# P*V with the query tiles split over the array's column halves, and the output projection in row tiles of 64

## What is computed

```python
h = _layernorm(x, ln1_g, ln1_b)
q = (xq @ wq).reshape(B, S, N_HEADS, D_HEAD)
k = (xkv @ wk).reshape(B, T, N_HEADS, D_HEAD)
v = (xkv @ wv).reshape(B, T, N_HEADS, D_HEAD)
attn = jnp.einsum("bihd,bjhd->bhij", q, k) * scale
attn = jax.nn.softmax(attn, axis=-1)
out = jnp.einsum("bhij,bjhd->bihd", attn, v).reshape(B, S, D_ATTN)
x = out @ wo + bo + x
```

## Time and profile before

| | us |
|---|---|
| three timed runs | 1082.41, 1084.62, 1083.84 |
| their median | 1083.84 |
| the profiled execution | 1080.77 |
| its span, first to last instruction | 1079.0 |
| TensorE, matmuls (weight loads) | 1032.9 (837.2) |
| VectorE | 832.9 |
| ScalarE | 623.0 |
| GpSimd | 307.8 |

### The profile page before, as it was taken

The page is one execution under the profiler, slowest core; times in us unless marked ns, Lnnn a source line. Parts: engine busy times, 40 slices in busy tenths (PEclk is TensorE's granted clock), DMA queues, the critical chain, the costliest instruction groups (busy, mean ns, idle before and its releaser), DMA issues.

```text
span 1079.0 us, 28600 instructions
## 1 busy us (share of the span) xinstructions
PE 1032.9 (96%) x12270; PEld 837.2 (78%) x12270; DVE 832.9 (77%) x977; ACT 623.0 (58%) x1120; POOL 307.8 (29%) x280
## 2 busy tenths in 40 slices
PE   6899999999998999999999999998999998999998
PEld 5677777777776777777777777776688888888887
DVE  3598888789989877878888889999868897655433
ACT  2566666566676655666666566676655643443322
POOL 2302332222332223423223222322313357701000
PEclk9999999999999999999999999999999999999999
DMA  7798677556755956665875666598210001100001
GB/s 155 189 219 169 155 151 172 124 114 134 162 114 113 204 114 147 131 133 124 162 159 121 145 122 147 116 218 174 46 60 20 1 20 41 39 1 20 21 1 40
DMA packets 178367, 121.39 MB, mean 113 GB/s; under 512 B 142656, under 2 KB 158528, under 8 KB 173760
## 3 DMA queue, kind: packets, MB, share of 16 engines
q1 hardware_dynamic: 177280, 116.40, 49.4%
q0 software_dynamic: 960, 3.15, 1.0%
HBM read 56.60 MB, written 12.58 MB: 64 GB/s over the span
## 4 chain that ended last, share of the span: by engine, by line
PE 80%; DVE 6%; ACT 5%; issue 4%; POOL 2%; SPq 1%; DMA 1%; DVEq 0%; ACTq 0%; POOLq 0%
PE W L628 21%; PE SC L603 18%; PE W L640 9%; PE SC L692 8%; PE W L578 8%; PE W L702 4%; PE W L588 4%; PE W L868 3%; ACT OTF L954 2%; PE SC L680 2%; DVE PR L1179 2%; DVE nmax L1174 2%; ACT PR L946 1%; PE W L855 1%; POOL PR L515 1%
## 5 line engine op out<-in xcount | busy, mean ns | idle before, releaser
L946 ACT ACTIVATE PR<-SC,nmax 128x1024 f32<-128x1024 f32 x256 | 285.9, 1117 | 225.0 <-DVE nmax L1174 224.5
L1174 DVE TENSOR_REDUCE nmax<-SC 128x1 f32<-128x1024 f32 x256 | 308.0, 1203 | 98.6 <-PE SC L603 97.9
L1179 DVE STREAM_TRANSPOSE PR<-PR 128x1024 f32<-128x1024 f32 x256 | 315.1, 1231 | 0.3 <-ACT PR L946 0.2
L603 PE MATMUL SC<-QKS 128*128 128x512 f32 x1024 | 297.4, 417 | 11.5 <-ACT PR L946 8.0
L464 POOL TENSOR_TENSOR X<-f_raw,X 128x512 f32<-128x512 f32 x128 | 164.8, 1289 | 496.0 <-ACT f_raw L965 495.9
L628 PE MATMUL W<-PR,V 32*64 32x256 f32 x8192 | 240.9, 379 | 1.9 <-issue 1.9
L603 PEld LDWEIGHTS SC<-QKS 128*128 128x128 f32 x1024 | 184.3, 188 | 72.2 <-issue 25.7
L628 PEld LDWEIGHTS W<-PR,V 32*64 32x64 f32 x8192 | 185.8, 132 | 50.8 <-issue 23.9
L640 PE MATMUL W<-wo,OTF 128*128 128x256 f32 x512 | 134.4, 385 | 7.3 <-ACT OTF L954 6.4
L640 PEld LDWEIGHTS W<-wo,OTF 128*128 128x128 f32 x512 | 93.9, 189 | 36.5 <-ACT OTF L954 20.3
L965 ACT ACTIVATE f_raw<-W,rden 128x256 f32<-128x256 f32 x256 | 106.8, 474 | 0.1
(11 more groups left out here) (127 smaller groups left out, 1416.9 us busy)
## 6 DMA issues: line engine op xcount, KB each, us to landing
QKS<-QKT SPq DMA_DIRECT2D x64, 512.0 KB, 6.3
V<-scratch_v SPq DMA_DIRECT2D x128, 256.0 KB, 5.0
QKS<-QKT SPq DMA_DIRECT2D x128, 128.0 KB, 4.9
scratch_v<-VST SPq DMA_DIRECT2D x32, 256.0 KB, 4.7
wo<-in_L_xattn_sa_wo_dram SPq DMA_DIRECT2D x64, 64.0 KB, 3.0
f_raw<-in_L_xattn_ff_w_dram POOLq DMA_DIRECT2D x12, 256.0 KB, 3.4
X<-in_x_dram SPq DMA_DIRECT2D x4, 512.0 KB, 5.0
w_raw<-in_L_xattn_sa_wk_dram SPq DMA_DIRECT2D x16, 128.0 KB, 3.5
```

Of the source, the lines that this page charges most:

```text
L603: last = mm(SC[t % 2][:, cols], QKS[:, 3 * s, t * P:(t + 1) * P], QKS[:, 3 * s + 1 + l, cols], start=(l == 0), stop=(l == 1))
L946: nc.scalar.activation(PR[:, NT * s + t, :], SC[t % 2][:, :], ACT.Exp, bias=nmax[:, t % 4:t % 4 + 1], accum_out=den[:, s, t:t + 1]).then_i ...
L1174: V.tensor_reduce(nmax[:, t % 4:t % 4 + 1], SC[t % 2][:, :], AX, ALU.max, negate=True).then_inc(d_max, 1)
L1179: V.transpose(tile, tile).then_inc(d_tr, 1)
```

## The change

P*V: each key block makes its products twice, once for each column half c of the array, and half c handles the query tiles 4c to 4c+3, 128 columns. All key blocks add up in both halves, so there are no even and odd sums any more: partitions 0 to 63 hold tiles 0 to 3 and partitions 64 to 127 tiles 4 to 7. `OTF` shrinks to 128x512. The projection then takes 64 rows of `OTF` and of `wo2` for each query tile, from partitions 0 to 63 for tiles 0 to 3 and 64 to 127 for tiles 4 to 7. Each of its two steps has four products, tiles t and t+4 in turn, which write two banks. Step 0 stands behind score tile 5, step 1 behind tile 7 and the projections there. ScalarE scales both results of step 0 ahead of the exponentials of tile 6. The pair of tiles that result k holds is now `OUT_TILE[k]`, and behind the last head the banks and waits of `make_vw` follow the new order of the scalings.

```diff
-        OTF = sb("OTF", [P, S])
+        OTF = sb("OTF", [P, BANK])
...
-        MB = [MISC, PV, TP[0], TP[1]]
+        MB = [PV, TP[1], TP[0], MISC]
...
-        STEPS = {5: 0, 6: 1, 7: 2}
-        OUT_BANK = (2, 1, 0, 1)
+        STEPS = {5: 0, 7: 1}
+        OUT_TILE = (0, 4, 2, 6)
+
+        def out_bank(h, n):
+            return (2, 1, 0, 3 if h == HS - 1 else 1)[n]
...
                 for blk in range(*blocks):
-                    cols = slice(DH * (blk % 2), DH * (blk % 2) + DH)
-                    for a in range(4):
-                        rows = slice(Q * a, Q * a + Q)
-                        last = mm(W[cols, a, 0:2 * P], V4[s][rows, blk, :],
-                                  PR[rows, NT * s:NT * s + NT, Q * blk:Q * blk + Q],
-                                  start=(blk < 2), stop=(blk >= NB - 2), tile_position=(Q * a, DH * (blk % 2)))
...
+                    for c in range(2):
+                        cols = slice(DH * c, DH * c + DH)
+                        tiles = slice(NT * s + 4 * c, NT * s + 4 * c + 4)
+                        for a in range(4):
+                            rows = slice(Q * a, Q * a + Q)
+                            last = mm(W[cols, a, 0:P], V4[s][rows, blk, :], PR[rows, tiles, Q * blk:Q * blk + Q],
+                                      start=(blk == 0), stop=(blk == NB - 1), tile_position=(Q * a, DH * c))
...
-            def project_out(h, k):
-                if k == 0:
+            def project_out(h, step):
...
                 for i in range(2):
-                    t = 2 * k + i
-                    last = mm(W[:, OUT_BANK[k], D * i:D * i + D], OTF[:, t * P:(t + 1) * P], wo2[h % 2][:, :],
-                              start=True, stop=True)
-                last.then_inc(s_op, 1)
+                    t = 2 * step + i
+                    for c in range(2):
+                        rows = slice(DH * c, DH * c + DH)
+                        last = mm(W[:, out_bank(h, 2 * step + c), D * i:D * i + D], OTF[rows, t * P:(t + 1) * P],
+                                  wo2[h % 2][rows, :], start=True, stop=True)
+                        if i == 1:
+                            last.then_inc(s_op, 1)
...
-                    if t == 0 and h > 1:
-                        pe.wait_ge(a_op, 4 * (h - 2) + 2)
-                        project_out(h - 2, 3)
...
+                    if h > 0 and t == 7:
+                        pe.wait_ge(a_op, 4 * (h - 1) + 2)
+                        project_out(h - 1, STEPS[t])
...
-                if j > 0:
-                    pe.wait_ge(a_op, 4 * (HS - 1) + (0, 1, 3, 4)[j])
+                pe.wait_ge(a_op, 4 * (HS - 1) + j + 1)
                 make_vw(0, j, MB[j])
...
-                               W[:, :, 0:2 * P].rearrange("p a (t i) -> p a t i", i=Q)).then_inc(a_ot, 1)
+                               W[:, :, 0:P].rearrange("p a (t i) -> p a t i", i=Q)).then_inc(a_ot, 1)
...
-                act.wait_ge(s_op, n + 1)
+                act.wait_ge(s_op, 4 * h + 2 * (k // 2) + 2)
...
-                    if t in (6, 7) and h > 0:
-                        scale_out(h - 1, t - 6)
+                    if t == 6 and h > 0:
+                        scale_out(h - 1, 0)
+                        scale_out(h - 1, 1)
                     if t in (0, 1) and h > 1:
                         scale_out(h - 2, 2 + t)
```

More of the change, by code:

```diff
@@ L462, in add_out @@
                         pool.wait_ge(p_xb, 2 * (h // NH) + 2)
-                    xs = X[:, h // NH, 2 * k:2 * k + 2, :].rearrange("p t d -> p (t d)")
+                    xs = X[:, h // NH, OUT_TILE[k]:OUT_TILE[k] + 2, :].rearrange("p t d -> p (t d)")
                     nc.gpsimd.tensor_tensor(xs, f_raw[:, k % 2, :], xs, ALU.add).then_inc(p_x, 1)
@@ L624, in attend @@
                 for blk in range(*blocks):
-                    cols = slice(DH * (blk % 2), DH * (blk % 2) + DH)
-                    for a in range(4):
-                        rows = slice(Q * a, Q * a + Q)
-                        last = mm(W[cols, a, 0:2 * P], V4[s][rows, blk, :],
-                                  PR[rows, NT * s:NT * s + NT, Q * blk:Q * blk + Q],
-                                  start=(blk < 2), stop=(blk >= NB - 2), tile_position=(Q * a, DH * (blk % 2)))
-                        if blk >= NB - 2:
-                            last.then_inc(s_pv, 1)
-            def project_out(h, k):
-                if k == 0:
+                    for c in range(2):
[5 more added lines that the diff above has]
+                                      start=(blk == 0), stop=(blk == NB - 1), tile_position=(Q * a, DH * c))
+                            if blk == NB - 1:
+                                last.then_inc(s_pv, 1)
+            def project_out(h, step):
+                if step == 0:
                     pe.wait_ge(a_ot, h + 1)
@@ L735, in _ @@
                         attend(h - 1, BURSTS[t])
-                    if h > 0 and t in STEPS:
+                    if h > 0 and t == 5:
                         project_out(h - 1, STEPS[t])
@@ L781, in _ @@
                         turn_wq(i, bank)
-                    if t == 0 and h > 1:
-                        pe.wait_ge(a_op, 4 * (h - 2) + 2)
-                        project_out(h - 2, 3)
-            pe.wait_ge(a_op, 4 * (HS - 2) + 2)
-            project_out(HS - 2, 3)
+                    if h > 0 and t == 7:
+                        pe.wait_ge(a_op, 4 * (h - 1) + 2)
+                        project_out(h - 1, STEPS[t])
             pe.wait_ge(m_kb[0], 16)
@@ L799, in _ @@
             ca_scores(1)
[L800 to L803, removed]
+            for step in range(2):
+                project_out(HS - 1, step)
             pe.wait_ge(m_vb[0], 16)
@@ L965, in scale_out @@
                     done = nc.scalar.mul(f_raw[:, k % 2, D * i:D * i + D],
-                                         W[:, OUT_BANK[k], D * i:D * i + D],
-                                         rden[:, h % 2, 2 * k + i:2 * k + i + 1])
+                                         W[:, out_bank(h, k), D * i:D * i + D],
+                                         rden[:, h % 2, OUT_TILE[k] + i:OUT_TILE[k] + i + 1])
                 done.then_inc(a_op, 1)
```

## The result

The changed kernel takes 1257.3 us, the median of four timed runs, beside 1083.12 for the kernel before on the same chip: a ratio of 1.162 (95% interval 1.158 to 1.167). It is slower by 16%, where the prediction said 2% faster. The profiled execution took 1259.82 us, 1258.0 of them the span.

What follows compares the result with a forecast made beforehand. TensorE was taken to set the pace, with VectorE close behind. From the profiled 1080.8 us, 27 gained in and behind the heads and 7 lost to instruction fetching gave 1060.8, or 1064 for the median; range 1042 to 1112.

Steps and rivals of the forecast that it cites:

- part 5: Fetching TensorE's added P*V instructions in 16 KB pieces: 7 us lost, with bounds of nothing and 166 us.
- Rival 3: Instruction supply too slow in P*V bursts: 1102 us at 8 ns an instruction, 1275 at 13.5; chance 0.20.
- Part 4: P*V bursts as 32 rounds of 128 columns, 3.42 to 3.57 us: +0.04 a burst, +0.08 a head.
- Parts 1 to 3: TensorE no longer waits for the copy; projection 1.72 us a head, was 3.44; array shape changes cost 0.8.
- the walk: Timeline of a plain head: next burst 1.0 us earlier, 0.9 to 1.0 gained with P*V; 23 over 24 heads.
- Rival 2: ScalarE or VectorE set the pace sooner in the heads: 0.3 to 0.4 us a head, 1078 us; chance 0.11.
- rival 4: The projection's 64-row tiles don't overlap: 1.72 us more a head, 1113 us; chance 0.05.

Runs made afterwards that it cites:

- cols256: The changed kernel with P*V's products at 256 columns again, over only the first half of the key blocks (the other half left out); 1067.63 us, ratio 0.987.
- no_qk_moves: The changed kernel without the transfers that move q and k from QKT to QKS from head 6 on; 1194.79 us, ratio 1.105.
- double_columns: The changed kernel with 256 columns in every P*V product, all key blocks and as many instructions; doesn't compute the function; 1315.66 us, ratio 1.218.

## Why the prediction was wrong

**What failed: part 5, the supply of instructions.** I had the 97 pieces and the 162 to come, saw four stalls that "may well stand where a piece begins", and priced a beginning within a burst at its average, 0.08 us, doubling the sum to 7. The stalls measured 131 us of idle time, 2.0 us for each of the 65 instead of 0.08, toward the upper bound of 166 that I gave and didn't believe. The average was the wrong reading: such a wait is nothing as long as the time between two beginnings covers it, and beyond that point the whole rest of it. What I should have worked out is the time from one beginning within P*V to the next, 5.4 to 5.5 us before and 1.85 after, and what the trace of before shows of the time that the next piece needs. It was there: the beginning at 380.5 stands 4.84 us behind the one before, by the numbers of the records, and TensorE was idle ahead of it (0.57). So that piece had taken 4.8 us to come, the other three that stalled 5.9, 6.1 and 7.4, and the change was about to ask for one in 1.85. The 2,029 instructions that I counted between two of the stalls are 2,048 with the 19 waits among them, 8 x 256 exactly; "may well" could have been "do".

**Rival 3 had the right sign and the wrong mechanism.** I framed it as a rate, 13.5 against 6.8 ns an instruction, argued against it with 24 instructions begun in 0.10 us, and took it to decide at 7.4 ns. That reading was beside the point: instructions that are there are begun fast. A burst start says nothing on what happens 256 instructions later. Its figure at the old rate, 1275, is close to what came, by a piece in 3.4 to 5.3 us instead of 1.85, not by a slower engine.

**The clock was not in the sum at all.** The granted clock is 0.955 where it was 0.993. Against cols256, the changed kernel loses 190 us (191 by the spans): 128 idle ahead of P*V (132.2 less 4.3), 45 in P*V's busy time (288.4 less 243.5) and 22 in the score tiles' (313.7 less 291.4), the last for the most part the lower clock behind long stalls; of these 195, 6 come back as a shorter wait ahead of the score tiles (25.4 to 19.5). How much of the 45 is the clock too isn't separated; in no_qk_moves, where it hardly falls in the heads, P*V is still busy for 275.2.

**Part 4, P*V** was mis-sized too. The typical round of eight matmuls takes 0.111 us, the upper of my two rows, but some are longer: 256 instructions, 16 rounds, take 1.85, so a burst of 32 is 3.70 and not 3.42 to 3.57. With the starts behind stalls the busy time grows by 0.54 a burst in no_qk_moves (275.2 less 240.9, over 64), where I had 0.04. That alone is 1.1 us a head, more than the 0.84 that the rest of the change gains; without stalls the restarts would be gone too, so how much of it would stay isn't shown.

**Parts 1 to 3 and the walk held.** The tiles of 64 rows overlap fully: a step of eight takes 1.06 us in the chain (0.20 + 0.86 in the walk) and the score tile behind it 1.14 by the same chain (0.20 + 0.93); the wait for the exponentials of tile 5 is 0.37 (0.4). A plain head of cols256 gains 0.84 us, where the walk without P*V's term has 1.0. What was wrong is the rest: 16 heads gain that much, not 24, and the other fifteen, among them those that wait for LayerNorm, the turns of x or single stalls, lost 2.4 us together, where I had a gain for all. Behind the last head nothing was won either (275.1 us from the last P*V to the end, 275.3 before). So 14 us where I had 27. Rival 2 didn't come: in cols256 VectorE's transposes hold up P*V three times, for 1.1 us in all. Nor did rival 4.

**Two rules that I had weighed.** The Trainium skill, TensorE: Matmul & The Clock Gate, section "Wait — 56ns, not 53.3ns?", has matmuls start no closer than about 25 ns. The trace of the changed kernel has 256 instructions, 128 matmuls among them, in 1.85 us over and over, 14.5 ns a matmul: for matmuls on eight different tiles the rule doesn't hold, and its 1247 us came close by chance. The Trainium skill, Runtime: NRT & Kernel Launch, section "Instruction fetch mechanics", gives TensorE room for 2,048 instructions; the same section says that the sequencer fetches "the next page while executing the current one" and that the cost is "mostly hidden". The trace agrees with the one page ahead, 256 instructions, and with nothing deeper; it contradicts "mostly hidden" with 0.7 to 5.8 us of idle time, 2.0 on average, at each of 65 pages in this kernel. I had weighed the depth and not the sentence beside it.

## What to carry to other kernels

Count the instructions of TensorE, waits included, where it sets the pace, and compare the time of each stretch of 256 with what the stalls here took: 3.4 us in quiet, and 5.2 on average but up to 8 beside heavy transfers. A change that halves the columns of every matmul may run into this though TensorE's own work shrinks. If the kernel before has even a few idle stretches in the middle of dense work, number its instructions and see where they stand before giving them an average price. And when a part of a step (here the copy) is made shorter, ask which wait ends last behind it: moving one projection step behind the next score tile won 6 us with the old layout, and the new layout's 14 came only with P*V at its old count of instructions.

## What the runs showed of the hardware

Where TensorE stalls, the packet with its next 256 instructions follows the beginning of the current ones: 0.9 us later in quiet and 3.1 us later on average (1.9 to 5.5, 14 stalls) when the DMA engines are over 90% busy, and the instructions start some 2.5 us after it. What delays the packet, the request or its place behind others, was not separated. That a transfer of q and k by SyncE makes TensorE's instructions late, and through them lowers its clock for two score tiles, I had not expected: with these moves gone the mean granted clock went from 0.955 to 0.981, with the long pieces of double_columns to 0.994. 64-row tiles side by side cost nothing beyond the change of shape: a step of eight instructions takes 1.06 us where the four of 128 rows took 0.86, and the score tile behind it 1.14 instead of 0.93.
